# Another order of all engines inside a batch, two searches by signs, and the second expert's weights in other buffers

## What is computed

```python
x = x + attention(layernorm(x), ctx, ctx, mask, WQ, bQ, WK, bK, WV, bV, Wp, bp)
h = layernorm(x)                                    # the expert's input
probs = softmax((layernorm(h) * ln_gamma + ln_beta) @ Wr + br)    # 8 experts
a = |w|; thr_bot = sort(a)[k-1]; thr_top = sort(a)[n-k]           # k = 5% of n
perturbed w = w + 0.8 * w * (-1 where a >= thr_top, +1 where a <= thr_bot, else 0)
out = probs[0] * ffn(h, clean) + (1 - probs[0]) * ffn(h, perturbed)
x = x + out                                         # ffn = gelu(h W1 + b1) W2 + b2
```

## Time and profile before

| | us |
|---|---|
| median of 3 runs | 751.48 |
| lowest and highest | 751.09, 755.43 |
| the profiled execution | 758.23 |
| its span, first to last instruction | 756.4 |
| PE busy in it | 672.9 (89%) |
| DVE busy | 517.6 (68%) |
| ACT busy | 381.6 (50%) |
| POOL busy | 272.6 (36%) |
| granted clock of PE, mean | 0.914 |

### The profile page before, as it was taken

The page is one execution under the profiler, slowest core; times in us unless marked ns, Lnnn a source line. Parts: engine busy times, 40 slices in busy tenths (PEclk is TensorE's granted clock), DMA queues, the critical chain, the costliest instruction groups (busy, mean ns, idle before and its releaser), DMA issues.

```text
span 756.4 us, 15501 instructions
## 1 busy us (share of the span) xinstructions
PE 672.9 (89%) x5555; PEld 613.3 (81%) x5555; DVE 517.6 (68%) x1205; ACT 381.6 (50%) x490; POOL 272.6 (36%) x284
## 2 busy tenths in 40 slices
PE   1758869999999399999999999999929999999996
PEld 1647858899889399889889899888828888898886
DVE  2778786786798869889888777653993445443452
ACT  2445226746747255855855855645304444445442
POOL 2343461673573358367366346325700000000000
PEclk9876577998999699999999998799959999999998
DMA  4996302622722440560640550231102221122221
GB/s 148 205 197 143 55 31 83 116 51 86 136 53 79 86 84 29 142 108 30 153 93 28 129 92 29 85 112 72 41 0 84 84 83 38 58 71 83 83 56 28
DMA packets 131797, 63.62 MB, mean 84 GB/s; under 512 B 104603, under 2 KB 122021, under 8 KB 131749
## 3 DMA queue, kind: packets, MB, share of 16 engines
q1 hardware_dynamic: 121652, 60.43, 32.9%
q10 hardware_dynamic: 10096, 2.56, 1.8%
HBM read 35.69 MB, written 23.09 MB: 78 GB/s over the span
## 4 chain that ended last, share of the span: by engine, by line
PE 67%; DVE 18%; issue 5%; SPq 4%; DMA 2%; ACT 2%; ACTq 0%; POOL 0%; DVEq 0%; POOLq 0%
PE ps_m L654 7%; PE ps_l L355 7%; PE ps_y L355 7%; PE ps_y L356 7%; PE ps_y L357 7%; PE ps_l L357 6%; PE ps_l L356 6%; PE ps_m L732 4%; DVE ind L1455 4%; PE ps_s L622 4%; PE ps_s L642 3%; DVE region_b L1430 3%; PE ps_m L694 2%; PE ps_s L355 2%; PE ps_s L357 1%
## 5 line engine op out<-in xcount | busy, mean ns | idle before, releaser
L996 ACT ACTIVATE region_b<-ps_l,bias 128x512 f32<-128x512 f32 x128 | 88.0, 687 | 172.5 <-PE ps_l L357 170.5
L355 PE MATMUL ps_y<-w_hi,region_c_hi 128*128 128x256 f32 x512 | 149.0, 291 | 0.0
L356 PE MATMUL ps_y<-w_lo,region_c_hi 128*128 128x256 f32 x512 | 146.7, 286 | 0.0
L357 PE MATMUL ps_y<-w_hi,region_c_lo 128*128 128x256 f32 x512 | 145.9, 285 | 0.0
L355 PE MATMUL ps_l<-x2s_hi,w_hi 128*128 128x512 f32 x256 | 108.8, 425 | 15.4 <-DVE x2s_lo L1314 14.8
L1237 POOL TENSOR_TENSOR region_c_lo<-region_b,region_c_hi 128x512 fp32r<-128x512 f32 x64 | 94.5, 1482 | 66.6 <-ACT region_c_hi L999 66.6
L1800 DVE TENSOR_TENSOR region_c_lo<-region_b,region_c_hi 128x512 fp32r<-128x512 f32 x64 | 44.3, 693 | 96.5 <-ACT region_c_hi L999 96.5
L357 PE MATMUL ps_l<-x2s_hi,w_lo 128*128 128x512 f32 x256 | 103.1, 403 | 0.0
L356 PE MATMUL ps_l<-x2s_lo,w_hi 128*128 128x512 f32 x256 | 102.9, 402 | 0.0
L356 PEld LDWEIGHTS ps_y<-w_lo,region_c_hi 128*128 128x128 f32 x512 | 98.6, 193 | 2.1
L355 PEld LDWEIGHTS ps_y<-w_hi,region_c_hi 128*128 128x128 f32 x512 | 98.5, 192 | 2.0
(11 more groups left out here) (200 smaller groups left out, 1228.1 us busy)
## 6 DMA issues: line engine op xcount, KB each, us to landing
qs<-q_scr SPq DMA_DIRECT2D x16, 512.0 KB, 6.5
acc_scr<-acc SPq DMA_DIRECT2D x8, 514.0 KB, 5.0
acc<-acc_scr SPq DMA_DIRECT2D x8, 514.0 KB, 3.4
xa<-in_x SPq DMA_DIRECT2D x8, 512.0 KB, 5.6
q_scr<-qn_lo SPq DMA_DIRECT2D x16, 256.0 KB, 5.0
x<-in_x SPq DMA_DIRECT2D x32, 128.0 KB, 3.9
xt_scr<-region_b SPq DMA_DIRECT2D x8, 512.0 KB, 2.6
region_b<-x SPq DMA_DIRECT2D x8, 512.0 KB, 3.1
```

The source lines that it names most:

```text
L355: eng.matmul(out_ap, a[0], b[0], start=first, stop=False)
L356: eng.matmul(out_ap, a[0], b[1], start=False, stop=False)
L357: return eng.matmul(out_ap, a[1], b[0], start=False, stop=last)
L996: act.activation(g[:, f % 4, :], ps_l[:, f % 2, :], ACT.Gelu_apprx_tanh, bias=bias[:, e, f:f + 1]).then_inc(s["gelu"].handle, 1)
```

## The change

- The credits are given by all five engines, each a fifth of the 86.
- Of the four large searches DVE and PE keep two; ACT sums the signs of the other two (`sum_signs` with s = 2 and 3). `counts` reads two of each.
- The order of the calls in `body` is another one on PE, DVE, ACT and POOL. On ACT all four exponentials and the router's now stand side by side, ahead of the GELUs. `second_round` is in parts: `end_first_round`, `lower_keys(0)`, `lower_keys(1)` and `start_second_round`, with other work between. In the last body ACT, not POOL, writes the second normalisation.
- The raw weights are loaded again into the `ind` tiles as soon as the last step's total is there, the magnitudes and marks go into the `key` tile, and the perturbed weights into buffers that attention no longer needs (`w1p` in qs and kbd, `w2p` in xhT and qn). Half of W1 is perturbed in the last body after the second normalisation's statistics, its other half ahead of that body's `mix`; W2, both biases and the low parts come in `last_expert`, between the low parts of the clean expert's activations, which DVE now makes. ACT writes the high parts after the second and the seventh GELU.
- The perturbed expert takes batch 7 first, whose input and accumulator are still in place (they are neither stored nor loaded), then batches 0 to 6.
- In the prologue each step has one compare and one count less, `top_scores(1, 3)` is earlier, and the rest stands as it was.

The diff, cut to its core and shifted left; `POOL`'s order is told after it.

```diff
-    wagain = view(region_a, 0, 2, WN)
-    tier = view(region_a, 2 * WN, WN)
+    wagain = [[ind[2 * n + h][:].bitcast(F32) for h in range(2)] for n in range(2)]
+    mag, tier = (key[:, 2 * n:2 * n + 2].rearrange("p a n -> p (a n)").bitcast(F32) for n in range(2))
+    w1p = [qs[:].rearrange("p m s -> p (m s)"), kbd[:].rearrange("p n m h k -> p (n m h k)")]
+    w2p = [[t[:].rearrange("p c s -> p (c s)") for t in pair] for pair in (xhT, qn)]
...
+def give(eng, share):
+    for s in signals[share::5]:
+        eng.sem_inc(s.handle, s.per)
+    give(sp, 0)
+    give(pe, 1)
-    for s in signals:
-        pool.sem_inc(s.handle, s.per)
...
-        sp.dma_start(wagain[:, 0].rearrange("p (c f) -> p c f", c=DC), W1.rearrange("(c p) f -> p c f", p=P)).then_inc(ld_again[0], 16)
-        sp.dma_start(wagain[:, 1].rearrange("p (c d) -> p c d", c=FC), W2.rearrange("(c p) d -> p c d", p=P)).then_inc(ld_again[1], 16)
+        wait(sp, total_ready, sum(BITS) - 1)
+        for h in range(2):
+            sp.dma_start(wagain[0][h], W1[h * P:(h + 1) * P, :]).then_inc(ld_again[0], 16)
+        for h in range(2):
+            sp.dma_start(wagain[1][h].rearrange("p (c d) -> p c d", d=D),
+                         W2.rearrange("(c p) d -> p c d", p=P)[:, h * FC // 2:(h + 1) * FC // 2]).then_inc(ld_again[1], 16)
+    if not last:
-    load_batch(0)
-    put_expert(B - 1)
+    load_batch(1)
+def batch_of(q):
+    return q - 1 if not isinstance(q, int) or q else B - 1
...
     h(1)
-    count(p, 2)
+    total(p)
     turn_probs(i, 1, last)
     values(i, 0)
-    total(p)
     if not last:
         queries(i + 1)
     c(0, 0)
     values(i, 1)
     turn_probs(i, 2, last)
+    h(2)
     c(0, 1)
-    h(2)
-    c(0, 2)
     turn_probs(i, 3, last)
     values(i, 2)
     h(3)
+    values(i, 3)
+    o(0)
+    turn_output(i)
     t(0)
-    values(i, 3)
     h(4)
-    turn_output(i)
-    o(0)
     o(1)
...
     c(1, 1)
-    s(0, 1)
     h(6)
-    s(1, 0)
-    c(1, 2)
-    s(1, 1)
-    h(7)
     t(1)
     o(2)
+    s(0, 1)
+    h(7)
     turn_x2(i)
     o(3)
+    s(1, 0)
+    s(1, 1)
+    r(0)
+    o(4)
     s(2, 0)
     c(2, 0)
-    r(0)
     c(2, 1)
+    s(2, 1)
+    s(3, 0)
+    t(2)
     r(1)
-    c(2, 2)
-    s(2, 1)
+    s(3, 1)
     r(2)
-    s(3, 0)
-    o(4)
+    o(5)
     r(3)
-    o(5)
-    t(2)
-    s(3, 1)
     o(6)
     o(7)
...
-def sum_signs(k, rnd):
+def sum_signs(k, rnd, which=(2, 3)):
-    act.activation(ind[3][:], key[:, key_of[rnd][3], :], ACT.Sign, bias=cand[:, 3:4], scale=-1.0,
-                   accum_out=signs[:]).then_inc(signs_summed.handle, 1)
+    for s in which:
+        act.activation(ind[s][:], key[:, key_of[rnd][s], :], ACT.Sign, bias=cand[:, s:s + 1], scale=-1.0,
+                       accum_out=signs[:, s - 2:s - 1]).then_inc(signs_summed.handle, 1)
...
     k = step_of(i, rnd)
         if (n or not turn) and not (n and last):
-            sum_signs(k + n, rnd)
+            sum_signs(k + n, rnd, which)
     turned(i, 0)
-    probs(i, 2)
     if not last:
         high_queries_input(i + 1)
+    probs(i, 2)
+    probs(i, 3)
     router_exp(i - 1)
+    turned(i, 1)
     more_gelu(0)
-    turned(i, 1)
-    more_gelu(1)
     if not last:
         high_queries(i + 1)
-    probs(i, 3)
+    more_gelu(1)
     turned(i, 2)
-    cmp(0)
+    cmp(0, 2)
     turned(i, 3)
     more_gelu(2)
+    cmp(0, 3)
+    high_output(i)
     more_gelu(3)
-    high_output(i)
-    more_gelu(4)
     if turn:
         act.wait_ge(key_ready, 16)
         act.wait_ge(state_ready, NS + 12)
-    cmp(1)
+    cmp(1, 2)
+    more_gelu(4)
+    cmp(1, 3)
     more_gelu(5)
+    if last:
+        wait(act, ln[1]["shift"], i)
+        for t in range(NT):
+            act.activation(xh[1][:, t, :], x2[:, t, :], ACT.Identity, bias=shiftby[1][:, t:t + 1],
+                           scale=rstd[1][:, t:t + 1]).then_inc(ln[1]["xhat"].handle, 1)
+    cmp(2, 2)
     more_gelu(6)
     copy_x2(i)
-    cmp(2)
+    cmp(2, 3)
     more_gelu(7)
     high_x2(i)
     if not last:
         probs(i + 1, 0)
+    cmp(3, 2)
+    cmp(3, 3)
+    if not last:
         probs(i + 1, 1)
-    cmp(3)
     router_exp(B - 1)
     for f in range(FC):
         gelu(0, B - 1, f)
+        if f == 1:
+            act.wait_ge(pw_ready, 2)
+            for h in range(2):
+                act.activation(w1p[0][:, h * F:(h + 1) * F], wagain[0][h], ACT.Copy).then_inc(pw_hi, 1)
+        if f == 6:
+            act.wait_ge(pw_ready, 4)
+            for h in range(2):
+                act.activation(w2p[0][h], wagain[1][h], ACT.Copy).then_inc(pw_hi, 1)
 pipeline(act, body, last_expert)
 act.wait_ge(pb_ready, 2)
...
+def lower_keys(n):
+    dve.wait_ge(key_ready, 8 + 2 * n)
+    for s in range(2):
+        dve.tensor_scalar(ind[s][:].bitcast(U16), key[:, n, :], prefix[:, 2 * n + s:2 * n + s + 1], 65535.0,
+                          ALU.not_equal, ALU.mult).then_inc(key_mark, 1)
+    dve.wait_ge(key_mark, 3 + 2 * n)
+    dve.tensor_tensor(key[:, n, :], ind[0][:].bitcast(U16), key[:, 2 + n, :], ALU.max).then_inc(key_ready, 1)
...
+def mark_tiers(w, m, tr, s):
+    limit = thr[:].rearrange("p s two -> p (s two)").bitcast(F32)
+    done_then(dve.tensor_scalar(m.bitcast(U32), w.bitcast(U32), 0x7FFFFFFF, None, ALU.bitwise_and))
+    done_then(dve.tensor_scalar(tr, m, limit[:, s:s + 1], -2.0, ALU.is_ge, ALU.mult))
+    done_then(dve.scalar_tensor_tensor(tr, m, limit[:, s + 1:s + 2], tr, ALU.is_le, ALU.add))
+def apply_tiers(dst, w, tr, done):
+    done_then(dve.tensor_scalar(tr, tr, -1.0, SCALE, ALU.max, ALU.mult))
+    dve.scalar_tensor_tensor(dst, tr, 1.0, w, ALU.add, ALU.mult).then_inc(done, 1)
+def mark_weights(n, h):
...
+    counts(p)
     if not last:
         low_queries_input(i + 1)
-    top_scores(i, 3)
-    counts(p)
     decide(p)
     if turn:
-        second_round()
+        end_first_round()
     cmp(0, 0)
     normalise_output(i, 0)
+    probabilities(i - 1)
+    cmp(0, 1)
     if not last:
         low_queries(i + 1)
-    cmp(0, 1)
-    normalise_output(i, 1)
-    cmp(0, 2)
-    probabilities(i - 1)
+    if turn:
+        lower_keys(0)
     if not isinstance(i, int) or i + 2 < B:
         wait(dve, x_in, i + 2)
         stats(0, i + 2, xa)
+    normalise_output(i, 1)
+    normalise_output(i, 2)
+    base(0, i - 1)
+    if turn:
+        lower_keys(1)
+    normalise_output(i, 3)
     cnts(0)
-    normalise_output(i, 2)
-    normalise_output(i, 3)
-    base(0, i - 1)
     dec(0)
     low_output(i)
-    cmp(1, 0, 1, 2)
+    if turn:
+        start_second_round()
+    cmp(1, 0, 1)
     add_residual(i)
     stats(1, i, x2)
-    masks(0)
     cnts(1)
+    dec(1)
+    if last:
+        thresholds()
+        mark_weights(0, 0)
+        perturb_weights(0, 0)
+    mask_one(0, 0)
+    mask_one(0, 1)
+    cmp(2, 0, 1)
     masks(1)
-    dec(1)
-    cmp(2, 0, 1, 2)
-    masks(2)
+    mask_one(2, 0)
     cnts(2)
-    logits(i)
+    mask_one(2, 1, False)
+    dec(2)
+    mask_top(2)
     mask_one(3, 0)
     mask_one(3, 1, False)
-    dec(2)
+    cmp(3, 0, 1)
     low_x2(i)
-    cmp(3, 0, 1)
+    logits(i)
+    mask_top(3)
+    if last:
+        mark_weights(0, 1)
+        perturb_weights(0, 1)
     mix(0, i - 1)
-    cmp(3, 2)
-steps = [0]
...
+    low_gelu(0, B - 1, 0)
+    mark_weights(1, 0)
+    low_gelu(0, B - 1, 1)
+    perturb_weights(1, 0)
+    low_gelu(0, B - 1, 2)
+    low_weights(0)
+    low_gelu(0, B - 1, 3)
+    mark_weights(1, 1)
+    low_gelu(0, B - 1, 4)
+    perturb_weights(1, 1)
+    low_gelu(0, B - 1, 5)
+    dve.wait_ge(pw_ready, 4)
+    perturb_hidden_bias()
+    low_gelu(0, B - 1, 6)
+    perturb_output_bias()
+    low_gelu(0, B - 1, 7)
+    low_weights(1)
```

242 lines of the change are left out of this document (126 added, 116 removed).

## The result

The changed kernel takes 731.3 us (median of four runs, 725.9 to 732.7), the kernel before 753.1 (four runs, 751.1 to 755.4). The ratio is 0.970, with a 95% interval of 0.963 to 0.976: faster by 22 us. The forecast was 710, with a range of 695 to 729. The direction was right. The size was not: by the two profiled executions, 758.2 and 729.9, 28.3 us were gained where the sum had 41.7. A few executions of a kernel run over 1.5% slower than its fastest; ratios and their intervals leave these out, medians don't.

A forecast was written before the change was run, and what follows sets the result against it. PE was taken to bound the middle bodies. Terms 5.6 + 3.0 + 11.0 + 4.0 + 3.4 - 1.4 + 16.1 = 41.7 us, taken from the 751.5 median, gave 709.8, say 710; range 695 to 729.

The forecast's parts named there:

- Credits: Ahead of the first DMA: sharing the 86 increments by five engines saves 5.6 us, 1.5 instead of 7.1.
- The lower bound of 2.7: Credit increments before the first DMA: 2.7 us saved if other engines take three times POOL's pace per increment.
- Prologue: Six prologue steps each lose one compare and one count: 3.0 us saved, at most 7.9.
- at least nothing: Prologue's low end: no gain where ACT's second sum of signs, 2.1 us more on ACT, ends last.
- Bodies 1, 2, 4, 5, 6: Five bodies: 8.4 us from PE counts plus 2.6 from lower-clock stretches, together 11.0, from 0 to 18.3.
- sign of being wrong: Middle bodies lasting 57 us or more, where near 53 was expected, would show the prediction wrong.
- Turn body: Turn body: 12.0 us stall cut up rather than gone, fewer counts, less lower clock; 4.0 us saved, from 0 to 10.
- Two stalls of 4 to 7 us: Turn body: two PE stalls of this size expected where one of 12 was, from the two lower-key pieces.
- Last body: Last body: two counts, a 1.74 us compare wait and part of the lower clock go; 3.4 saved, from 0.8 to 7.
- Clean expert and between the experts: Clean expert 1.4 us longer; between experts 16.1 saved: 14.8 stall and 2.5 clock, less a 1.2 wait.
- Signs late: Rival, bodies: ACT's second sum ends after `counts` wants it, stalling DVE, then PE; slower, 769 us; chance 0.04.
- Only the ends gain: Rival: bodies keep their time, new small waits eat the counts; 24.3 us gained in all, 727; chance 0.22.

The follow-up runs named there:

- pool_tail_old: The changed kernel with only the second half of GpSimd's old body order (router's rsqrt before the next first shift, second shift behind both low parts): 711.3 us, ratio 0.944.
- port_probe: The changed kernel with VectorE compares and maxima timed alone or beside GpSimd work after its last work: compare 0.75 us alone, 2.71 beside TENSOR_TENSOR.

## Why the prediction was right or wrong, step by step

*Credits: the size was off.* The rows of GpSimd alone gave 5.6. It is 4.4 in the trace and 3.7 (1.1 to 6.2) by time, since TensorE needs 3.4 us for its share and all wait for it. The lower bound of 2.7 was made for that.

*Prologue: wrong, by all of its 3.0.* From the first turned probabilities of batch 0 to those of batch 1, which begin body 1, it takes 62.9 us now (from 52.1 on) and took 63.0 before; of the 4.9 gained, 4.4 are the credits'. The end that the prediction gave as "at least nothing" is the case. The chain of work that ended last, in the prologue of the changed kernel:

```profile
66.39 1.63 issue
68.04 0.24 issue
68.28 2.17 ACT ind L1002 x3
70.45 0.92 ACT region_a L1008
```

ScalarE starts the first sum at 66.37 and the second at 68.37, so the 1.63 and 0.24 of issue are the first one's time, and the turned probabilities (L1008) wait behind both. Between the same two points a second pair lies on the chain at 84.6, and others lie outside them, at 39.4 and 118.7; in the kernel before, no sum of signs is on the chain up to body 1. What the missing compares and counts gave is spent there.

*Bodies 1, 2, 4, 5, 6: the step that failed, by 14 us.* Its first terms were right: TensorE's work in a body fell by 2.0 us (busy for 54.3 of body 4 before, and 52.4 in pool_tail_old, both at full clock), ScalarE went to 41.4 of a body (forecast 42.4), and VectorE doesn't wait for signs. The low clock, of which 2.6 us were to come back, grew instead, from 21 to 30 us in the five bodies. Take the low clock as costing half of its length, and the busy and idle time of the five bodies add up to this: TensorE's own work 7.0 us less (a rough figure, as the 2.0 of a body at full clock would make it 10), slow clock 4.6 more (half of 9.2), idle time 5.4 more (10.6 after 5.2). Of the idle time now, 5.0 are the waits at `cnt` and the mask ahead of it, and 2.9 are one wait of body 1 for probabilities that stand behind the sums of the prologue's last step (L1008); gone are waits for a low part (L1374 of the kernel before), 3.7 in all. Four of the five bodies (61.4, 57.6, 57.5 and 57.0) stand at the 57 or more that the prediction named as its sign of being wrong. The failure is in what the step left out. I followed the new orders of ScalarE and VectorE, and GpSimd's not at all: its new order was costed at nothing, without naming what hides it. It moved a shift of 1.9 us under the compares of step 2. The prediction had the size of such a meeting in its own rows, 2.48 for a compare when GpSimd is at work and 2.17 for 1.22, used it for the turn, and did not ask where the new order makes new meetings. With the second half of GpSimd's order put back, the same five bodies last 59.6, 53.1, 53.4, 53.3 and 52.3, 14.2 us less than in the kernel before; forecast 11.0.

*Turn body: nearly right, for partly wrong reasons.* 2.9 gained, 4.0 forecast. Two stalls of 4 to 7 us were named. TensorE's waits there:

```profile
PE ps_m L683 <- DVE on L1419: 4.2, 1, 4.2
PE ps_m L775 <- DVE cnt L1525: 0.8, 2, 0.5
...
PE ps_s L695 <- DVE on L1419: 0.6, 1, 0.6
```

The first came (4.2). The second is 0.6: its half of the keys is hidden. In its place stands the collision of the other bodies, with a second stretch at the lower clock (0.90 over the body). Without the collision the body takes 61.7, 6.3 gained.

*Last body: under-sized.* 6.4 for 3.4. All of the lower clock went (1.00 now), where the sum took back 0.9 of the 4.7 us that it was worth. It lay within the bound of 7.

*Clean expert and between the experts: right, and a little better.* The clean expert takes 2.5 us more (forecast 1.4). TensorE waits twice for 0.8 us for a low part of the GELU (L1763), which stands once behind the applying of W2's second half and once behind the output bias. The gap of 14.8 is gone, the first output of the second expert doesn't wait, and VectorE's `mix` starts at 541.8, 3.3 us behind the last clean product. So the wait of 1.2 that was forecast didn't come. The second expert takes 4.7 less where 2.5 of clock less that wait were counted: part of the rest is that its other passes are 0.25 us shorter each, 22.92 for 23.17.

*The rivals.* "Signs late" (0.04) isn't what happened to this kernel, but it is what happens to the split in the old order, 766 us. That this is near the 769 of the prediction is chance: the 769 has 20.3 us of gains at the ends in it, which that run doesn't have. "Only the ends gain" (0.22) is closest to the result, 727 with the bodies near their old time. It spoke of VectorE that "slows when POOL works beside it", which is the mechanism. But it put a loss of counts there and no loss through clock.

*What stays open.* What brings the lower clock. In the changed kernel it stands beside the two waits at `cnt` in five bodies of six, and in pool_tail_old bodies 2, 4, 5 and 6 have neither. But the waits alone don't decide it. In the trace of port_probe, whose bodies are those of the changed kernel, bodies 5 and 6 have the same 1.0 us of waits and stay at full clock. Waits of 1.2 us at 178.6 and of 1.3 us at 502.9 of the changed kernel bring no lower clock either. And body 5 of the kernel before runs at 0.50 from 407.4 on, for 3.4 us, with no gap of TensorE over 0.1 us in the 9 us ahead. No run kept TensorE busy through the waits. So the 4.6 us of clock belong to the collision by their place alone; the waits themselves and the 13 to 20 us that went when the collision was taken away don't hang on it.

pool_tail_old, at 711.3, is the fastest version of all: 0.944 of the kernel before, 20 us under the changed one.

## What to carry to other kernels

When all engines' orders change together, follow each of them through the new order, also the one with the least work. GpSimd is busy for a third of the time here, and the place of one of its calls decided 13 us, the order of its second half 20. For each TENSOR_TENSOR of GpSimd ask what VectorE does beside it; where a meeting falls on VectorE's chain to TensorE, put small work or a wait in between. And the worth of a saved instruction belongs to the order around it: the same split cost 13 us in one order and gave 17 to 26 in others.
